# Walk of a graph kernel: where the opening and closing products stand, and how many PSUM banks hold sums

## What is computed

```python
def f(y):
    return jax.ops.segment_sum(y[src3] * e3, dst3, num_segments=N)
k1 = f(x)
k2 = f(x + dt * k1 / 3)
k3 = f(x + dt * (k2 - k1 / 3))
k4 = f(x + dt * (k1 - k2 + k3))
y = x + dt * 0.125 * (k1 + 3 * (k2 + k3) + k4)
...
x = _layernorm(x + _L1_gnn_ref(x, edge_attr3_4x1, src, dst), axis=-1)
```

## Time and profile before

| | us |
|---|---|
| median of 3 runs (3494.34 to 3498.09) | 3495.58 |
| the profiled execution | 3501.67 |
| its span, first to last instruction | 3499.9 |
| hop 0 in it, 1058 to 1553 | 495 |
| hop 3 in it, 2559 to 3100 | 541 |
| the walk in it, 3100 to 3492.4 | 392.4 |

### The profile page before, as it was taken

One profiled execution on the slowest core, in us unless ns is written; L12 is line 12 of the kernel. 1 busy time (PEld: TensorE's weight loads), 2 busy tenths in 40 slices (PEclk: granted clock), 3 DMA queues, 4 the chain that ended last, 5 costly groups with the idle time before them and its releaser, 6 DMA issues.

```text
span 3499.9 us, 31921 instructions
## 1 busy us (share of the span) xinstructions
PE 1189.6 (34%) x6041; PEld 999.4 (29%) x6041; DVE 2478.0 (71%) x6241; ACT 1452.2 (41%) x3372; POOL 2597.1 (74%) x2761
## 2 busy tenths in 40 slices
PE   4666664666661311101111101111100000047777
PEld 4555653544441211101111101111000000046776
DVE  7677616888888786657777767777769999943332
ACT  4445544666661222213333323333325555533333
POOL 7777766777757777767777767777767777748888
PEclk8777787788875555555555555555555555568888
DMA  5555585666653444436777767777757777777775
GB/s 134 172 167 176 175 174 159 217 211 213 215 193 114 147 138 151 147 121 220 252 255 241 248 202 243 247 253 254 237 180 261 263 260 259 264 215 196 197 205 142
DMA packets 423033, 710.22 MB, mean 203 GB/s; under 512 B 100050, under 2 KB 286734, under 8 KB 416592
## 3 DMA queue, kind: packets, MB, share of 16 engines
q1 hardware_dynamic: 235754, 474.50, 40.0%
q0 software_dynamic: 82128, 182.11, 19.2%
q10 hardware_dynamic: 104960, 51.58, 5.1%
HBM read 370.71 MB, written 337.25 MB: 202 GB/s over the span
## 4 chain that ended last, share of the span: by engine, by line
POOL 43%; issue 17%; DVE 14%; PE 8%; DMA 2%; ACT 2%; ACTq 0%; DVEq 0%; SPq 0%; POOLq 0%
POOL gs L1573 32%; POOL gs L834 10%; PE psum L1937 8%; DVE psum L1689 3%; DVE stats L1239 2%; DVE tn L1654 2%; DVE da L1699 2%; DVE psum L1670 2%; DVE new_res L1233 2%; ACT psum L1632 1%; DVE mv L1245 1%; DMA gs<-u,far_row 0%; PE psum L1919 0%; DVE last_z L1695 0%; DMA u<-cross,first_idx 0%
## 5 line engine op out<-in xcount | busy, mean ns | idle before, releaser
L1573 POOL DMA_INDIRECT gs<-u,far_row x1176 | 1115.4, 948 | 363.6 <-issue 357.4
L1133 PE MATMUL psum<-wu_i,d_xt 128*128 128x128 f32 (+1 forms) x782 | 210.9, 443 | 1100.0 <-DVE d_res L1165 1099.9
L1632 ACT ACTIVATE psum<-da 128x512 f32<-128x512 f32 x288 | 173.1, 601 | 888.3 <-DVE tn L1654 553.8
L1670 DVE TENSOR_TENSOR psum<-gs,psum 128x1024 f32<-128x1024 f32 x192 | 234.9, 1224 | 419.0 <-DMA gs<-u,far_row 285.1
L1133 PEld LDWEIGHTS psum<-wu_i,d_xt 128*128 128x128 f32 (+1 forms) x782 | 176.4, 326 | 1136.4 <-issue 1136.4
L343 POOL DMA_INDIRECT pt<-in_x_dram,idx x392 | 386.1, 985 | 123.6 <-issue 119.0
L834 POOL DMA_INDIRECT gs<-rows_e,edge_id x392 | 370.9, 946 | 141.4 <-issue 119.1
L1573 POOL DMA_INDIRECT gs<-x1s,far_row x392 | 374.2, 955 | 120.7 <-issue 119.1
L1689 DVE TENSOR_TENSOR_SCAN psum<-goes_on,psum 128x1024 f32<-128x1024 f32 (+1 forms) x200 | 447.5, 2238 | 0.6
L1909 DVE TENSOR_TENSOR hot<-pos,rel_s 128x1536 f32<-128x1536 f32 x66 | 125.4, 1903 | 255.3 <-ACT psum L1975 228.1
L1937 PE MATMUL psum<-ring,hot 128*128 x1584 | 292.4, 340 | 11.0 <-issue 1.6
(11 more groups left out here) (286 smaller groups left out, 3944.4 us busy)
## 6 DMA issues: line engine op xcount, KB each, us to landing
u<-da SPq DMA_DIRECT2D x144, 512.0 KB, 4.0
rows_e<-pt SPq DMA_DIRECT2D x48, 1056.0 KB, 4.7
total<-tn SPq DMA_DIRECT2D x98, 512.0 KB, 3.3
gs<-total SPq DMA_DIRECT2D x98, 512.0 KB, 5.9
fin_d<-normed SPq DMA_DIRECT2D x49, 516.0 KB, 4.9
ring<-fin_d SPq DMA_DIRECT2D x49, 516.0 KB, 4.7
gs<-u SPq DMA_DIRECT2D x49, 512.0 KB, 5.4
gs<-x1s SPq DMA_DIRECT2D x49, 512.0 KB, 6.4
```

The costliest lines, as they stand in the source:

```text
L1133: t = pe.matmul(d_new_psum[k % 2][0:P, r * D:(r + 1) * D], d_xt[k % 4][:, r * 128:r * 128 + P], wu_i[:, :], start=True, stop=True)
L1573: g.indirect_dma_start(gx[b % 4][:, j * D:(j + 1) * D], None, source[:, :], bass.IndirectOffsetOnAxis(ap=far_row[:, c:c + 1], axis=0)).the ...
L1632: act.mul(shared, half(us[b % 3], i), share).then_inc(shared_set, 1)
L1670: return v.tensor_tensor(zf.rearrange("p (h f) j -> p j h f", h=H), by_head(gxv(b % 4)[:, c0:c1, 0:D]), per_head(wt_rest[:, c0:c1, :] if b ...
```

## The change

1. Six banks hold sums in place of seven; idle openings and closings go to bank 6 for even triples and to bank 7 for odd ones. The table `need_b` becomes the group's last window less 4. The constant in the table of banks changes with it, and DVE clears 3072 columns of PSUM in place of 3584.
2. The opening product of a triple stands between the second and the third product of the triple before it, except for the first triple of a load of words, where it stands ahead. The closing product of a triple stands behind the first product of the next triple, except in the last triple of a group, where it stands at the end as before. PE's wait for a group's `hot` is taken where the triple begins.
3. The table of opening and closing places is computed for even and odd triples apart: five more small DVE operations in hop 0.
4. At the end of hop 3, `o_shifts(47)` stands between the last scan and `keep_last`, no longer between `o_rows(48)` and `o_statistics(48)`.

```diff
-SCRATCH = 7 * SLOT
+BANKS = 6
+SCRATCH = BANKS * SLOT
...
-                next_op(at + 29, need_b, by_group[1], -6.0, ALU.add, 0.0, ALU.max)
-                next_op(at + 30, need_b, need_b, float(base), ALU.add)
+                next_op(at + 34, need_b, by_group[1], -4.0, ALU.add, 0.0, ALU.max)
+                next_op(at + 35, need_b, need_b, float(base), ALU.add)
...
                 add_up_runs(i + 1)
+                if h == 3:
+                    o_shifts(v, b - 1)
                 keep_last(i + 1)
...
                     o_rows(v, b)
-                    o_shifts(v, b - 1)
                     o_statistics(v, b)
...
                         if tri % TRI_OF == 0:
                             pe.wait_ge(oh_set, base + g + 1)
-                        at = word[WORDS + tri]
-                        open_bank(bass.ds((at >> FIELD).with_bounds(min_val=0, max_val=SCRATCH + SPARE), 2))
+                        if tri == 0:
+                            open_bank(opens(word, tri))
                         for k in range(3 * tri, 3 * tri + 3):
                             pe.matmul(psum[:, bass.ds((word[k] >> FIELD).with_bounds(min_val=0, max_val=SCRATCH - D - 1), D + 1)],
                                       hot[g % OHS][:, k % GROUP, :],
                                       ring[:, bass.ds(word[k] & ((1 << FIELD) - 1), D + 1)], start=False, stop=False)
-                        close_bank(bass.ds((at & ((1 << FIELD) - 1)).with_bounds(min_val=0, max_val=SCRATCH + SPARE), 2))
-                last = (WIN3 - 1) % 7 * SLOT + SPARE
+                            if k % 3 == 0 and tri % TRI_OF > 0:
+                                close_bank(closes(word, tri - 1))
+                            if k % 3 == 1 and tri + 1 < WORDS // 3:
+                                open_bank(opens(word, tri + 1))
+                        if tri % TRI_OF == TRI_OF - 1:
+                            close_bank(closes(word, tri))
+                last = (WIN3 - 1) % BANKS * SLOT + SPARE
```

More of the change, by code:

```diff
@@ L1398, in places_vector, with every_other @@
             at += 13
+            def every_other(t):
+                return [t.rearrange("o (i k) -> o i k", k=2)[:, :, odd] for odd in range(2)]
             by_group = [t.rearrange("o (g k) -> o g k", k=GROUP)[:, :, GROUP - 1] for t in (block_at[0:1, :], third)]
@@ L1430, in places_vector @@
                 so_far(at + 16)
[L1431 to L1440 removed]
+                for odd in range(2):
+                    v.scalar_tensor_tensor(every_other(at_open)[odd], every_other(last_of[1])[odd], -float(SCRATCH + odd * SLOT),
+                                           every_other(moved)[odd], ALU.add, ALU.mult).then_inc(walk_set, 1)
+                    v.tensor_copy(every_other(at_close)[odd][:, 0:1], every_other(moved)[odd][:, 0:1]).then_inc(walk_set, 1)
@@ new lines, in places_vector @@
+                so_far(at + 20)
+                v.scalar_tensor_tensor(every_other(at_close)[0][:, 1:TRIS // 2], every_other(last_of[1])[1][:, 0:TRIS // 2 - 1],
+                                       -float(SCRATCH), every_other(moved)[0][:, 1:TRIS // 2], ALU.add, ALU.mult
+                                       ).then_inc(walk_set, 1)
+                v.scalar_tensor_tensor(every_other(at_close)[1], every_other(last_of[1])[0], -float(SCRATCH + SLOT),
+                                       every_other(moved)[1], ALU.add, ALU.mult).then_inc(walk_set, 1)
@@ new lines, in places_vector @@
+            if b == ROWB + 5:
+                for odd in range(2):
+                    next_op(at + 22, every_other(at_open)[odd], every_other(at_open)[odd],
+                            float(SCRATCH + odd * SLOT + SPARE), ALU.add)
+                    next_op(at + 22, every_other(at_close)[odd], every_other(at_close)[odd],
+                            float(SCRATCH + odd * SLOT + SPARE), ALU.add)
+                next_op(at + 26, at_open, at_open, FIELD, ALU.logical_shift_left)
+                so_far(at + 27)
```

35 lines of the change are left out of this document (15 added, 20 removed).

## The result

The changed kernel takes 3503.44 us in the median of 11 runs (3495.77 to 3506.08), the kernel before 3495.12 us (3492.66 to 3498.09) beside it. The ratio is 1.0022, with an interval of 1.0013 to 1.0031. Forecast was 3496.6 us. So the loss of about 8 us sits at the 0.2% bound of "no change", and the median lies 0.4 us above the upper end of the range, 3503.

A forecast was written before the change was run, and what follows sets the result against it. The prediction took PE's sequencer to bound the walk and POOL to bound hop 0. Its terms, 0.8 + 0.1 + 0.1 = +1.0 us on the median of 3495.58, gave 3496.6 us, with a range of 3491 to 3503.

The forecast's parts named there:

- Rival A: Walk: PE's execution sets the time and the split hides a weight load; 26 us faster, 3470 us; chance 5%.
- Order of the products: Walk, PE's sequencer: same 14 instructions per triple, no neighbour sets a price, so 264 x 0 = 0.
- rival D: Walk: new neighbours cost or save the sequencer 0.03 us or more per triple, 8 us, 3488 or 3504 us; chance 4%.
- the sequencer covers it: Walk: a triple executing 0.1 us longer, 0.9 us, hides behind 1.16 us of issue; uncovered it would cost 26 us.
- Six banks and `need_b`, +0.8 us: Walk: later `hot` builds make PE wait 0.7 us at group 9 and 0.1 us at group 5.
- Rival B: Walk: evictions become the bound; 3 us later throughout gives 13.6 us of waits, 3509 us; chance 6%.
- Clearing of PSUM, 0: Walk's start: clearing is shorter by a seventh of 3 us, but the first `ring` load releases PE later: 0.
- hop 3's end, +0.1 us: Hop 3's end: moved shifts save 0.10 us at the statistics and cost 0.16 us at the copy.
- Hop 0, +0.1 us: Hop 0: more small DVE operations slow POOL's gathers, which set the stage; +0.1 us, bounds 0 and 0.5 us.
- Rival C: Walk: PE stays at the lower clock level through whole loads; 10 us slower, 3506 us; chance 3%.
- the neighbours' 2.1 us: Walk: bound either way if new neighbours changed one instruction's issue by a tenth in each of 264 triples; taken as 0.
- stalls of 3 us: Walk: the forecast range's allowance for early stalls, 0 to 3 us.

The follow-up runs named there:

- e_f32_close: The kernel before with each closing product in fp32, two PE passes for one, and one more column of zeros: 3538.71 us, ratio 1.0117.
- e_by_group: The kernel before with opening and closing places as words of their own, 66 loads of 20 words, one register operation fewer per triple: 3485.55 us, ratio 0.9971.
- the pair with constants: e_const_before and e_const_after: the kernel before and the changed kernel, both with ACT's and DVE's limits as constants: ratios 1.0004 and 1.0015.
- e_close_moved: The changed kernel with only closing products between steps, each opening ahead of its own triple again: 3500.53 us, ratio 1.0014.
- e_old_order: The changed kernel with PE's products in the order of before; banks, limit, tables and moved shifts stay: 3500.52 us, ratio 0.9998.
- c_before: The kernel before, unchanged, run again for a second profile: 3498.65 us, ratio 0.9997.
- e_need4: The kernel before with only the limit of `need_b` at the last window less 4, not 6; seven banks stay: 3499.14 us, ratio 0.9997.
- e_shifts: The kernel before with only the shifts of batch 47 moved ahead of `keep_last` at hop 3's end: 3499.78 us, ratio 0.9999.
- e_const_before: The kernel before with ACT's and DVE's limits as constants in place of register loads: 3500.24 us, ratio 1.0004.
- e_f32_half: The kernel before with every other closing product in fp32: 3497.1 us, ratio 1.0004.
- the first five: Profiles of the kernel before, c_before, e_old_order, e_need4 and e_shifts: mean walk 395.0 us, with 78.7 us of loads.
- e_no_ring: The changed kernel without ring transfers from the ninth on, 41 of 49 missing, and without SP's waits for them: 3497.46 us, ratio 1.0007.
- e_const_after: The changed kernel with ACT's and DVE's limits as constants in place of register loads: 3504.03 us, ratio 1.0015.

## Why the prediction was right or wrong

**What bounds the walk.** Right: the sequencer does. Issue of the products is 308 to 310 us in every kernel with its 14 instructions per triple but e_f32_close, whatever the clock (0.79 to 0.84), and e_by_group, with one instruction fewer, is faster by 0.29%. Rival A, that PE's execution binds and the split shortens it, is out: PE's execution got longer (a triple 0.19 us at the lower level, 0.08 us at the higher), not shorter.

**Order of the products, "264 x 0 = 0".** As a price of the sequencer the term holds: the distances between its instructions are the same in both orders (0.092 us from the first register operation to the second, 0.162 us from a step's address to the next), and so is the issue sum. So rival D is out. What failed is the sentence beside it, that a triple may execute 0.1 us longer and "the sequencer covers it". It covers it in a triple at the higher level, not over a load of words. Eight triples at the lower level are 13.8 us (12.2 us in the old order) where the period is 11.9, and at the higher level PE now gains 0.27 us per triple on the sequencer (1.16 less 0.89) and no longer 0.35. So in over a third of the loads PE is still 0.8 to 1.9 us behind when the next load of words begins; with PE's program of before it is 0.1 us behind as a rule, 0.8 us at most. I had compared 0.9 with 1.16 us at the higher level only, although the 1.53 us of the lower level stood in the earlier trace rows. Such a backlog costs little by itself, since the load's 2.4 us absorb it. The time is in the loads of words, which I had taken as fixed: 33 loads sum to 83.3 us, not 78.7 us. That is the mis-sized term, 0 forecast, 4.6 us by these means (1.7 us by the pair with constants). The forecast of no clear change came close all the same, but by luck: the +1.0 us is made of other terms, and a loss of this kind was in none of them.

**Of this, what is shown and what is not.** Shown: the loss goes with the order. The three runs of it and e_close_moved are slower by 0.14 to 0.22%, each with an interval that excludes no change; of the five in the old order with one pass per closing (e_old_order, c_before, e_need4, e_shifts, e_const_before) none is. In the walk's parts it is mostly in the loads. Not shown is by which property of the order: small products apart, a longer execution by PE, or closings that come later and shift the evictions and transfers with them. The longer execution alone, in e_f32_half (six tenths of it), costs nothing that can be measured. Nor is it shown what lengthens the loads. If the backlog does, it explains, by 12 loads x 0.127 us, some 1.5 us of the 4.6. By the DMA engines' share more loads meet ring transfers, 48% and not 32%: 33 x 0.16 x 0.25 us = 1.3 us; by time under way no more do. And e_const_before has 2.3 us more of loads than the mean of the first five with neither the order nor a backlog, so part of the 4.6 us may be a spread whose cause is unknown. At least 2 us stay open. Beyond the walk's 5.2 us, the first measurement has another 3 us that nothing here places. e_no_ring can't settle it: without transfers the change is at +0.07%, with an interval that takes in no change, but there is no run of the old order without transfers to compare with.

**Six banks and `need_b`, +0.8 us.** Right in size, within its spread. Two of DVE's builds early in the walk and one late, in the changed kernel:

```profile
3127.24 1.92 DVE L1922 TENSOR_TENSOR hot<-pos,rel_s 128x1536 f32<-128x1536 f32 x1 [3.49 <-ACT psum L1999]
...
3150.86 1.76 DVE L1922 TENSOR_TENSOR hot<-pos,rel_s 128x1536 f32<-128x1536 f32 x1 [6.69 <-ACT psum L1999]
...
3370.69 1.87 DVE L1922 TENSOR_TENSOR hot<-pos,rel_s 128x1536 f32<-128x1536 f32 x1 [3.53 <-ACT psum L1999]
```

The build of 3127.24 is group 5's. It ends at 3129.16 and PE's sequencer goes on at 3129.19, 0.50 us after its operation before, where 0.12 us is usual: a wait of 0.4 us. In the second profile the same place has 0.99 us, a wait of 0.9 us; in e_const_after it has 0.1 us, in e_close_moved 0.7 us, and group 9 has 0.8 us there. So 0.1 to 0.9 us with the change's order and limit, where I said 0.8, but at group 5, to which I gave 0.1 us, and not at group 9: one piece, not two to four. Later groups don't wait, as forecast for number 47; from number 11 on the builds start 5.3 us ahead of their use in the median (11.7 us in the kernel before), as forecast. Rival B, evictions that bind throughout, is out. The rows of waits name five pieces with 10.1 us for `hot`; the others stand at loads of words, where PE would have paused for the load anyway: the sequencer's own records have no waits there, so the piece belongs to the load.

**Clearing of PSUM, 0; hop 3's end, +0.1 us.** Both nothing that can be measured; the shifts cost 0.15 us at the copy and give back 0.16 us at the statistics.

**Hop 0, +0.1 us.** The gather beside the four operations, and what DVE does, against the earlier trace rows:

```profile
1289.60 1.23 POOL L1585 DMA_INDIRECT gs<-x1s,far_row  x1 [0.30 <-issue]
1291.14 0.98 POOL L1585 DMA_INDIRECT gs<-x1s,far_row  x1 [0.30 <-issue]
...
1290.97 0.38 DVE L1436 SCALAR_TENSOR_TENSOR new_res<-tn,normed 1x132 int32<-1x132 int32 x1
...
1293.59 1.23 DVE L1682 TENSOR_TENSOR psum<-gs,psum 128x1024 f32<-128x1024 f32 x1 [1.12 <-DMA gs<-x1s,far_row]
```

The operation over 132 places takes the 0.38 us that I put, and DVE still idles ahead of the weighing, 1.12 us. One gather takes 1.23 us and the next 0.98, together 2.21 us. In the kernel before, the 1.10 us of the earlier trace rows are followed by

```profile
1293.60 1.01 POOL L1573 DMA_INDIRECT gs<-x1s,far_row  x1 [0.30 <-issue]
```

together 2.11 us: 0.1 us more, as forecast. The second profiles of both kernels have 2.13 us before and 2.07 us after, so even this isn't resolved, and over the stage POOL's busy time is 0.6 us less than before. By the Trainium skill ("SBUF — State Buffer", "Who interferes with whom") my estimate had been up to 0.5 us more blocking; neither pair of profiles shows that much.

**Rival C, a clock that stays low, 3%.** It didn't happen here, the grant is 0.83. But e_f32_close shows that it exists, a little further on: one pass of PE more per triple costs 41 us by its run, with the grant at 0.65. This rival deserved more than 3%. Its condition, "longer pauses or the split", was incomplete: in e_f32_close PE stays at the lower level for 30 us, from 3198.28 to 3228.21, without a pause. That shorter pauses go with a higher grant is seen too, 0.91 in e_by_group. What holds the level in either case stays open.

**Range and chances.** The range's upper end rested on the neighbours' 2.1 us, stalls of 3 us and the runs' spread of 3.7 us; added up straight these reach 3505.4 us, and I stopped at 3503. It had no term for the duration of the loads, though the earlier trace rows showed 2.13 to 2.80 us for the same 32 words, a spread of up to 22 us over 33 loads whose cause I hadn't looked for. The measured periods from load to load are 11.5 to 12.6 us, 12.04 in the mean, where the kernel before has 11.5 to 12.4 and 11.90.

## What to carry to other kernels

Cover is to be added up over the whole period, at the slower clock level too, and not triple by triple: an engine that runs just ahead of its sequencer has little to give, and here the loss showed in a step that had looked fixed. Where a sequencer bounds a loop, count register operations first: a table laid out so that an address comes straight from a word was worth 0.29%, even with twice as many loads. And when a bound has a part with an unexplained spread, that spread belongs into the range, and into the comparison afterwards: one more kernel of the old order, e_const_before, takes half off the difference in the loads when it is the one compared with.

## What the runs showed of the hardware

- Two small products with weights of their own cost more apart than side by side. By the distances from start to start at the lower level (1.2 GHz), a pass of a step takes 0.21 us, a small product behind another 0.07 us, the pass behind a small one 0.03 to 0.07 us, but then that step's second pass comes 0.36 us later: I read this as each lone small product leaving the next weight load uncovered by 0.14 us. At the higher level (2.4 GHz) these are 0.11, 0.03, 0.03 and 0.19 us, so 0.08 us. In sum a triple takes 1.72 us and not 1.53, or 0.89 and not 0.81.
- PE's sequencer is held when PE is far behind: 342 us of issue in e_f32_close for the instructions that take 308 us elsewhere. The Trainium skill ("TensorE: Matmul & The Clock Gate", section "Architectural detail: the array is 16× 32×32, not 1× 128×128") gives TensorE's queue 64 entries; the run agrees that the queue ends somewhere, its depth no run here shows.
- A load of 32 words into PE's registers takes 2.13 us at the least, one of 20 words 1.36 us: by my estimate from the two 0.064 us per word. With packets of a ring transfer on over 30% of the DMA engines' time it is 0.25 us longer in the mean (2.56 against 2.31 us), with a PE that is still executing 0.13 us longer, though not in the loads of 20 words; both go together with the load's length, and neither was shown to cause it. Without register loads of ACT and DVE at the time the loads get no shorter (81.0 us in e_const_before).
- Between two profiles of the same kernel the walk varied by 2.2 us, over six with PE's program of before by 3.9 us, and what lies ahead of it by up to 8 us. A change of 5 us in one stage is found in that stage's parts, not in spans.
